# Two edits around the last attention unit and in the expert stage of a four-layer kernel: the second layer norm of batches 4 and 5 is moved, and the experts' bias is added by GpSimd instead of TensorE

## What is computed

```python
x = x + tanh(g_xattn[0]) * cross_attention(layernorm(x), ctx)     # 32 heads, 8 kv heads
x = x + tanh(g_ffn[0])   * grouped_ffn(layernorm(x))              # perm, up, gelu, down, unperm
x = x + tanh(g_xattn[1]) * group_attention(layernorm(x), ctx)
x = x + tanh(g_ffn[1])   * experts(layernorm(x))

def grouped_ffn(x):            # 16 groups of 32 features
    t = x[:, perm].reshape(n, 16, 32)
    t = gelu(einsum('bhd,hdm->bhm', t, up))
    return einsum('bhm,hmd->bhd', t, down).reshape(n, 512)[:, argsort(perm)]

def experts(x):                # each token uses one of 8 experts
    sel = argmax(softmax(x @ gate_w.T + gate_b))
    return x @ expert_w[sel].T + expert_b[sel]
```

## Time and profile before

| | |
|---|---|
| median of three runs | 791.48 us (787.73 to 792.2) |
| the profiled execution: time | 789.23 us |
| the profiled execution: span, first to last instruction | 787.3 us |
| busy share of PE, DVE, ACT, POOL | 95%, 58%, 55%, 35% |
| mean granted TensorE clock | 0.986 of full speed |

### The profile page before, as it was taken

How to read it: one execution, slowest core, us unless ns; L and a number is a source line. 1 busy time by engine, 2 the same in 40 slices (tenths; PEclk the granted TensorE clock), 3 DMA queues, 4 the chain that set the end, 5 groups by cost and what they waited for, 6 DMA issues and landing times.

```text
span 787.3 us, 12378 instructions
## 1 busy us (share of the span) xinstructions
PE 747.2 (95%) x3847; PEld 587.2 (75%) x3847; DVE 456.2 (58%) x1006; ACT 431.1 (55%) x1274; POOL 275.2 (35%) x431
## 2 busy tenths in 40 slices
PE   6999989899999999999999999999999988887997
PEld 4788877688887878888878788888787743565775
DVE  4786412456465555564655555655558755887653
ACT  5553315556556556655655655655655557556831
POOL 0331005234325323424423523432322438714242
PEclk9999999999999999999999999999999999997999
DMA  8545461132041140140132203203132135754232
GB/s 303 190 130 174 133 191 42 47 155 81 15 175 31 64 175 28 54 185 16 67 113 88 67 29 161 81 14 122 34 122 96 55 107 167 287 243 151 82 110 78
DMA packets 42126, 87.82 MB, mean 112 GB/s; under 512 B 5561, under 2 KB 26041, under 8 KB 38226
## 3 DMA queue, kind: packets, MB, share of 16 engines
q1 hardware_dynamic: 38884, 78.71, 28.7%
q0 software_dynamic: 3184, 8.41, 3.1%
HBM read 70.28 MB, written 35.57 MB: 134 GB/s over the span
## 4 chain that ended last, share of the span: by engine, by line
PE 69%; DVE 5%; POOL 4%; DMA 3%; ACT 3%; issue 2%; POOLq 0%; SPq 0%; DVEq 0%
PE banks L881 8%; PE banks L883 7%; PE banks L882 7%; PE banks L915 7%; PE banks L917 7%; PE banks L916 7%; PE banks L867 7%; PE banks L902 3%; PE banks L894 2%; PE banks L1829 2%; PE banks L1830 2%; PE banks L1831 2%; PE banks L926 2%; PE banks L928 2%; PE banks L927 2%
## 5 line engine op out<-in xcount | busy, mean ns | idle before, releaser
L592 ACT ACTIVATE p_sb<-p_sb,nmax 128x128 f32<-128x128 f32 x256 | 99.7, 391 | 57.5 <-DVE nmax L784 57.4
L587 ACT ACTIVATE oT_hi<-banks 128x512 fp32r<-128x512 f32 x64 | 38.2, 596 | 135.0 <-PE banks L928 135.0
L821 DVE SCALAR_TENSOR_TENSOR x_sb<-banks,tgates,x_sb 128x512 f32<-128x512 f32 x64 | 47.9, 749 | 65.9 <-PE banks L917 65.9
L690 POOL TENSOR_TENSOR v_lo<-v_raw,v_hi 128x128 fp32r<-128x128 f32 x64 | 29.5, 460 | 127.7 <-ACT v_hi L635 127.7
L779 DVE SCALAR_TENSOR_TENSOR p_sb<-banks,q_rstd,mask 128x128 f32<-128x128 f32 x256 | 71.4, 341 | 2.9 <-POOL q_rstd L83 2.4
L695 POOL TENSOR_TENSOR p_sb<-p_sb,rsum 128x512 f32<-128x512 f32 x64 | 66.5, 1039 | 15.1 <-DVE rsum L811 15.1
L867 PEld LDWEIGHTS banks<-kT,qT_sb 128*128 128x128 f32 x512 | 67.7, 193 | 5.4
L867 PE MATMUL banks<-kT,qT_sb 128*128 128x128 f32 x512 | 68.2, 277 | 0.0
L768 DVE TENSOR_TENSOR oT_lo<-banks,oT_hi 128x512 fp32r<-128x512 f32 x64 | 44.1, 689 | 32.9 <-ACT oT_hi L587 32.9
L400 PE MATMUL banks<-w_hi,ctx_hi 128*128 128x512 f32 x128 | 54.1, 422 | 7.9 <-DVE ctx_lo L331 7.8
L811 DVE RECIPROCAL rsum<-prob_sum 128x4 f32<-128x4 f32 x64 | 11.3, 176 | 81.8 <-ACT p_sb L592 81.8
(11 more groups left out here) (276 smaller groups left out, 1888.7 us busy)
## 6 DMA issues: line engine op xcount, KB each, us to landing
sorted_x<-in_empty SPq DMA_DIRECT2D x8, 2064.0 KB, 11.2
w_raw<-in_wq_l SPq DMA_DIRECT2D x8, 1024.0 KB, 5.9
w_raw<-in_wo_l SPq DMA_DIRECT2D x8, 1024.0 KB, 4.8
exp_w<-in_exp_w_l SPq DMA_DIRECT2D x8, 1024.0 KB, 10.6
kT_scr<-kT_st SPq DMA_DIRECT2D x16, 256.0 KB
v_scr<-v_st SPq DMA_DIRECT2D x16, 256.0 KB, 2.3
xs<-sorted_x SPq DMA_DIRECT2D x15, 258.0 KB, 3.6
v_raw<-v_scr SPq DMA_DIRECT2D x14, 256.0 KB, 2.6
```

What stands on the lines that cost most here:

```text
L592: last = act.activation(p_sb[:, b % 2, h * P:(h + 1) * P], p_sb[:, b % 2, h * P:(h + 1) * P], ACT.Exp, bias=nmax[:, b % 2, h:h + 1], accum ...
```

## The change

**Batches 4 and 5.** Their layer norm is taken out of the start of `middle` and put into the drain, beside batches 6 and 7 of the attention: variance after batch 5 on DVE, seed on ACT, Newton on GpSimd, both normalisations on DVE, eight transposes on PE, one copy each on ACT and DVE. At the start of `middle` only batches 6 and 7 are left; DVE normalises and copies both. The scratch `xT_scr` and the gathers now go by thirds instead of halves, so that batches 4 and 5 are gathered by themselves (four more indirect DMAs, of half the width). GpSimd's first two `scale_ctx` stand behind that gather. PE does the first up product before the transposes of batches 6 and 7.

**The bias.** The matmul with the bias is gone from each tile. `exp_b` is multiplied by the gate early in the attention and stored once; in the experts stage SP loads it, broadcast to all 128 partitions, in two DMAs of 1 MB between the loads of the row tiles, and GpSimd adds the expert's row of it to `xs` (`add_bias`, after `normalise` has read the slot and before `add_y`). For the last seven tiles GpSimd reads the expert's number from the table into a register first. The split of the bias, its zero fill (ACT, L1520) and its load (L1466) are gone.

```diff
@@ attention: variance, and the new stages in the drain
-                    if b % HB == HB - 1:
-                        layernorm_var(dve, s, x_step, 2 * (b + 1), slice(b + 1 - HB, b + 1)).then_inc(xval_done, 1)
+                    if b in LN2_LAST:
+                        layernorm_var(dve, s, x_step, 2 * (b + 1), LN2_LAST[b]).then_inc(xval_done, 1)
+            def rstd_ln2_45(u, b, g, odd):
+                if after(u, b, g, HB + 1):
+                    pool.wait_ge(xseed_done, 2)
+                    newton_rsqrt(pool, xnewton, 3, s.xval[:, C45], s.xseed[:, C45], s.xtmp[:, C45], s.xrstd[:, C45],
+                                 s.c15).then_inc(xrstd_done, 1)
+            def normalise_ln2_45(u, b, g, odd):
+                if after(u, b, g, HB + 1):
+                    dve.wait_ge(xrstd_done, 2)
+                    for n in (HB, HB + 1):
+                        dve.tensor_scalar(xln2[:, n, :], s.x[:, n, :], mv[:, n, 0:1], s.xrstd[:, n:n + 1],
+                                          ALU.subtract, ALU.mult).then_inc(xln_done[1], 1)
...
             run(dve, ...
-                 (p_recip, 0), (accumulate, -2), (copy_xT, -4), (x_stats, -2)])
+                 (p_recip, 0), (normalise_ln2_45, -3), (copy_xT5, -4), (accumulate, -2), (copy_xT, -4), (x_stats, -2)])
...
-                [(scores, 0), (sum_squares, 4), (z01, 0), (p_transpose, -1), (z2, -1), (o_proj, -2),
+                [(scores, 0), (sum_squares, 4), (z01, 0), (p_transpose, -1), (z2, -1), (transpose_x45, -4), (o_proj, -2),
@@ middle: GpSimd
-            for c in range(2):
-                if c:
-                    pool.wait_ge(ctx_nat_ld, 16)
-                    pool.wait_ge(col_step, 2)
-                    scale_ctx(range(2))
-                pool.wait_ge(xT_stored[c], 32)
+            def gather(c):
+                lo, hi = THIRDS[c]
+                pool.wait_ge(xT_stored[c], 16 * (hi - lo) // 2)
                 for jt in range(KT):
...
+            gather(0)
+            gather(1)
+            pool.wait_ge(ctx_nat_ld, 16)
+            pool.wait_ge(col_step, 2)
+            scale_ctx(range(2))
+            gather(2)
             scale_ctx(range(2, 4))
@@ middle: ACT
             copy_z(4)
-            act.wait_ge(xval_done, 2)
...
+            copy_z(5)
+            act.wait_ge(xval_done, 3)
+            act.activation(xtmp[:, C67], xval[:, C67], ACT.Ln, scale=2.0).then_inc(xln_ln, 1)
+            act.wait_ge(xln_ln, 3)
+            act.activation(xseed[:, C67], xtmp[:, C67], ACT.Exp, scale=-0.5).then_inc(xseed_done, 1)
+            copy_z(6)
...
-            copy_z(5)
-            act.wait_ge(xshift_done, 1)
-            normalise2(5)
-            normalise2(7)
-            copy_xT(5)
-            copy_xT(7)
             act.preload_act_table(ACT.Gelu)
@@ middle: DVE
-            negated_shift(dve, s, H1, xrstd, xshift).then_inc(xshift_done, 1)
-            normalise2(4)
             normalise2(6)
-            copy_xT(4)
-            copy_z(6)
+            normalise2(7)
+            copy_z(7)
             copy_xT(6)
-            copy_z(7)
+            copy_xT(7)
@@ experts: SP
-            sp.wait_ge(bias_zeroed, 1)
-            sp.dma_start(s.exp_b2[0:2, :, :].bitcast(F32), d.exp_b2).then_inc(exp_b_ld, 16)
...
                 sp.dma_start(xs[:, slot, :], rows).then_inc(xs_ld[slot], 16)
+                if t in (1, 3):
+                    c = t // 2
+                    if t == 1:
+                        sp.wait_ge(x3_done, B)
+                    sp.dma_start(s.bias[:, BIAS[c], :], d.bias[:, BIAS[c], :]).then_inc(bias_ld[c], 16)
@@ experts: GpSimd
-            for t in range(TILES):
-                store(t)
+            pool.wait_ge(tile_done, 1)
+            found = [pool.value_load(tile_i[0:1, k:k + 1], min_val=0, max_val=E - 1) for k in range(EXTRA)]
+
+            def add_bias(t):
+                slot = t % SLOTS
+                pool.wait_ge(xn_done, t + 1)
+                if t in (0, HB):
+                    pool.wait_ge(bias_ld[t // HB], 16)
+                e = ORDER[t] if t < E else found[t - E]
+                pool.tensor_tensor(xs[:, slot, 0:D], xs[:, slot, 0:D], s.bias[:, e, :], ALU.add).then_inc(bias_added, 1)
+
+            run([(add_bias, 2), (store, 0)])
@@ experts: DVE and PE
                 dve.wait_ge(y_done, t + 1)
+                dve.wait_ge(bias_added, t + 1)
...
-                pe.matmul(out, s.ones_r[:, :], s.exp_b2[:, e, :], start=True, stop=False)
```

## The result

The changed kernel takes 793.48 us (median of 20 runs), the kernel before 790.1 us (20 runs beside them). The ratio is 1.0037, with a 95% interval of 1.002 to 1.0054: 2.9 us slower by the ratio, where 1.1 us faster was forecast. The time lies in the predicted range.

What follows compares the result with a forecast made beforehand. Pace was taken as set by the last store and GpSimd's last gather in the middle, and by PE, the store-load-normalise loop and DVE's splits in the experts; -2.1 + 1.0 = -1.1, giving 790.4 us on 791.48, range 786 to 795.5.

Steps and rivals of the forecast that it cites:

- (3): Middle, last store of transposed rows: lands in 3.0 to 3.3 us against 5.2, -1.9; gathers in flight +0.2.
- (1): Drain: variance after batch 5 on DVE ahead of `oT_lo`, +0.2 us; seed, Newton, normalisations and transposes taken as 0.
- (2): Batches 6 and 7: ACT's copy +0.5, Newton 0.5 to 0.6 back, DVE's copies 0.6 less; with (1) last store 0.4 earlier.
- (4): Experts: PE does 15 bias matmuls less, -3.5 us if PE stayed the bound.
- (5): Experts: first bias load ahead of tile 2 costs about 2.8 us on SP's queue, tile 1 +1.3.
- (6): Experts: GpSimd's additions and DVE's splits exclude each other; turns 4.4 instead of 3.66 us, +2.2 over three turns.
- (7): Experts: the loop carries the delay on, tile 12 2.0 us later; last three tiles gain 0.23 each; +1.0.
- No exclusion: Rival, experts: additions and splits don't exclude each other, turns stay 3.66 us; in all -3.2, 788.3 us; chance 0.2.
- PE stays the bound: Rival, experts: bias load fits in unnoticed, stores go out sooner; -3.5 - 2.1 = -5.6, 785.9 us; chance 0.15.
- slow bias load: Rival, experts: load at half the rate (5.6 us), tile 1 2.8 later, tile 4 another 2; 795.2 us; chance 0.15.
- The middle's rival: Middle gains nothing because the store is held up or GpSimd is late; +1.0, 792.5 us; chance 0.05.

Runs made afterwards that it cites:

- e7: The first edit alone plus 5 extra matmuls, result unread, in PE's wait ahead of the transposes of y; 785.88 us, ratio 0.9942 to before.
- e1: The kernel before with only the first edit (batches 4 and 5, thirds), the bias staying on TensorE; 790.88 us, ratio 0.9999.
- e15: The first edit alone, with the gathers of batches 4 and 5 issued only when the last store has landed; 795.22 us, ratio 1.0062 to before.
- e9: The second edit alone without any addition of the bias, its loads kept; 789.81 us, ratio 0.9989 to before.
- e14: Full change plus five extra matmuls, additions for tiles 4 to 7 behind DVE's splits, bias loads ahead of the scattered-rows wait; 785.82 us, ratio 0.9932 to before.
- e11: The second edit alone, additions for tiles 4 to 7 waiting until DVE has ended that turn's split; 789.8 us, ratio 0.9992 to before.
- e2: The kernel before with only the second edit (bias added by GpSimd), the middle as before; 793.87 us, ratio 1.0061.
- e13: The full change with five extra matmuls behind the second g product; 791.52 us, ratio 1.0008 to before.
- e8: The second edit alone without the additions for tiles 4 to 7; 789.48 us, ratio 0.9986 to before.
- e10: The second edit alone with both bias loads issued ahead of the wait for the scattered rows; 793.18 us, ratio 1.0037 to before.
- e6: The kernel before with four g products moved into PE's wait ahead of the first transposes of y; 788.1 us, ratio 0.9976.
- e3: The first edit alone plus 16 extra matmuls, result unread, in PE's wait ahead of the transposes of y; 797.98 us, ratio 1.0086 to before.

## Why the prediction was wrong

It was wrong in its direction and by 4.0 us in its size (forecast -1.1, measured +2.9), and both halves of the sum had a part.

**The step that failed in the middle** is behind (3): "From the last gather to 669.71 GpSimd's list is the same, so 2.1 arrives there, and the rest of the middle follows with it." It didn't follow. The prediction had said of the FFN that it could end 4 us earlier "and nothing would be won", and hadn't asked what its earlier end costs: PE's wait grows from 2.5 to about 5 us, and the work behind it runs at the lower granted clock for longer: 23.3 us "behind" instead of 21.6 on average, and 19.2 with the wait covered (e7). That took back the gain (e1: 0.9999). The profile before showed the low clock behind the shorter wait (0.52 and 0.62), and the prediction had no term for it.

**Terms of the middle.** (1) holds: +0.2, PE's wait for `oT_lo` in the drain was 0.47 instead of 0.25, and eight transposes, seeds and normalisations cost nothing. (2) holds about: counted from the last accumulation the last store went out 0.9 earlier (643.8 - 637.4 against 643.48 - 636.17), where 0.6 was forecast ((2) without the 0.2 of (1)). (3) was mis-sized: landing 4.8, not 3.3 and 0.2 for the disturbance. The gathers of batches 4 and 5 were in flight beside it; they went from 639.7 to 644.5 and not from 637.5 to 642.5, since their own store landed at 639.4 only. Whether they made the last store slow is open (e15). In all the first edit brings the transposes of y 1.0 us forward in the changed kernel and 1.3 in e1, and in e7, where the store landed in 3.8 us, the forecast's 2.1 came about (31.4 instead of 33.5).

**The experts.** (4) was rightly left out of the sum: PE isn't the bound. With no addition at all (e9) and 15 bias matmuls less the experts take 53.0 us, not less than the 52.0 of before, and with the loads ahead as well and the additions timed (e14) 51.7, where 15 matmuls are 3.5. DVE's turns of 3.66 in the splits and then the loop of store, load and normalisation set the pace. (5) is about right: tile 1 came 4.1 us behind tile 0 instead of 3.5, forecast 4.5, and in the other runs with these loads between the rows 4.2 to 5.4 (e11, e2, e9, e13, e8). e10 prices the loads at 1.5 to 1.9 us, forecast 1.3. (A load of 1 MB at the 298 to 351 GB/s of the earlier trace rows would be 3.0 to 3.5 us, not 2.8.) (6) had the mechanism right and the size wrong. The prediction let the addition start when the split was over ("split 2.4, the rest of the store 0.86, addition 1.15, next split: 4.4"), so that most of it would have gone beside DVE's two operations on PSUM. In fact GpSimd comes between DVE's four operations, the split itself is stretched from 2.49 to 4.02, and these two operations come behind it: 5.2 a turn. That is 1.55 more than before, four times, 6.2 us, where the step had 2.2 over three turns. (7), which says "2.0 later" and adds up 1.7, carried it on: its +1.0 for the experts was +5.4 in the profiles (57.4 to 51.95), and the runs of e2 give +4.8.

The Trainium skill says in "SBUF — State Buffer", section "Who interferes with whom", that a DVE instruction with two SBUF inputs contends with a GpSimd one that reads SBUF, that one with at most one such input does not, and that the shared port pair is an exclusive lock. (That the first keeps it to its end, as the prediction has it, the section says of DVE's two-port modes.) The additions agree with all three: beside DVE's reads of PSUM nobody waits (e11), and beside a split they take 1.3 us as alone, while DVE stands up to 2.24 us in one operation. Its inference that descriptor generation is not held up by `tensor_tensor` doesn't agree: in e8 three of four stores beside splits took 2.46 us and one 1.27, where those outside took 0.97 to 1.02. The prediction had from this inference that the experts would come out at about 0. They came out at +4.8, but by the additions, on which the section is right.

In "TensorE: Matmul & The Clock Gate", section "Part 1: The HAM clock gate", it says that the lower level of the clock is what idleness brings, and that the moment of a change also hangs on a phase that no kernel sets. The runs agree with the first (0.50 behind the waits of 2.5 to 5.6 us ahead of the transposes of y, and 1.00 in e7, where 0.45 us of wait is left); the second no run here shows. The page was not used for the forecast, and it speaks against "the rest of the middle follows".

**The rivals.** "No exclusion" and "PE stays the bound" are refuted by e2 and e9. The slow bias load was priced at half the rate, and tile 1 came 0.6 us later in the changed kernel and at most 1.9 in the others (e8). The middle's rival, no gain there, was given 0.05 and is what happened, though not for its reasons. That the time lies in the predicted range is luck: by e1 and e2 the middle came out 2 us worse than forecast and the experts 4, and the range had been made wide for a slow bias load, which didn't come.

## What to carry to other kernels

When an edit lets an engine finish earlier ahead of a fixed arrival, ask what its longer idle does to the granted clock behind it; if the work there is on the path, put work into the gap, its own if there is some, and look where the next gap then opens. An operation of GpSimd that shuts out DVE's two-input operations is cheap or dear by its moment alone: beside DVE's reads of PSUM the four additions cost nothing, beside the splits 5 to 6 us. And removing work from an engine is worth nothing while a loop through other engines has the same pace.

## What was not expected of the hardware

- The same wait costs more in one execution than in another: with waits of 2.5 to 3.0 us and the same middle (before, e2, e8, e10, e11) "behind" took 20.6 or some 22.3 us. The phase that the Trainium skill names (above) would do this; no run here shows that it is the cause.
- What PE waits for varies too: from the start of the last scatter of the first third to the transposes of y it took 8.3 to 8.7 us in most profiles where PE stood waiting, but 9.8 in e2, 10.1 in e9 and 10.7 in e6. GpSimd's list there is the same in all of them; the cause is open.
- A store beside a split takes 2.46 us and leaves the split at 2.49 (e8), or takes 1.41 and the split 2.62 (e11), though both start 0.9 us into it. In e11 an addition had ended 0.6 us earlier. Why this changes who waits was not settled.
- A float32 matmul of 128x512 takes 0.87 us in e3 (13.90 for 16), and one with the operands split into high and low parts 0.23 for each of its three.
